# Expert stage of a six-layer decoder on one core: norm, gates and routing moved among the first shared tiles

## What is computed

```python
xn = _layernorm(x)                                  # per row
logits = xn @ gate_w.T                              # 8 experts
topk_w, topk_i = top_k(softmax(logits), 2)
topk_w = topk_w / (topk_w.sum(-1) + 1e-20) * 2.5
y = sum over the 2 chosen e of topk_w * (silu(xn @ w_gate[e]) * (xn @ w_up[e])) @ w_down[e]
out = x + y + shared_1(xn) + shared_2(xn)           # the same form of MLP, 352 wide each
```

## Time and profile before

| what | value |
|---|---|
| median of 3 runs | 4069.13 us (4068.13 to 4070.47) |
| time of the profiled execution | 4078.57 us |
| its span, first to last instruction | 4076.8 us |
| mean granted TensorE clock | 0.928 |
| busy share PE, DVE, ACT, POOL | 86%, 72%, 63%, 46% |
| this stage | from 3479.9 us of the span to its end |

### The profile page before, as it was taken

The page is one execution under the profiler, slowest core; times in us unless marked ns, Lnnn a source line. Parts: engine busy times, 40 slices in busy tenths (PEclk is TensorE's granted clock), DMA queues, the critical chain, the costliest instruction groups (busy, mean ns, idle before and its releaser), DMA issues. The chain is left out here.

```text
span 4076.8 us, 64192 instructions
## 1 busy us (share of the span) xinstructions
PE 3499.0 (86%) x22125; PEld 2796.1 (69%) x22128; DVE 2930.9 (72%) x5974; ACT 2550.4 (63%) x3361; POOL 1863.8 (46%) x1143
## 2 busy tenths in 40 slices
PE   6867623369999999999999999995889889679999
PEld 4645421247777777877778788773767667579999
DVE  4568789868878887788878888884666675434347
ACT  2334445448878887787878878872666666234433
POOL 0034410026555565565555556532766666380005
PEclk9988856689999999999999999996999999699999
DMA  1047700058878888787878878880748559432224
GB/s 49 0 94 131 143 1 1 1 139 151 143 139 147 140 149 140 139 153 139 143 138 142 151 143 155 154 155 18 134 88 152 102 91 176 166 122 90 76 77 144
DMA packets 1571360, 470.22 MB, mean 115 GB/s; under 512 B 1507174, under 2 KB 1565159, under 8 KB 1569767
## 3 DMA queue, kind: packets, MB, share of 16 engines
q1 hardware_dynamic: 1564903, 449.40, 58.0%
q0 software_dynamic: 6144, 16.79, 1.2%
HBM read 49.00 MB, written 39.58 MB: 22 GB/s over the span
## 5 line engine op out<-in xcount | busy, mean ns | idle before, releaser
L2299 DVE TENSOR_REDUCE d_neg_max<-psum 128x1 f32<-128x1024 f32 x512 | 625.1, 1221 | 249.9 <-PE psum L2040 244.1
L2189 ACT ACTIVATE psum<-psum,d_bias 128x1024 f32<-128x1024 f32 x512 | 557.6, 1089 | 336.0 <-DVE d_bias L2303 332.2
L2040 PE MATMUL psum<-d_KH,d_QH 128*128 128x512 f32 x2048 | 682.7, 415 | 19.7 <-DVE d_halves L2308 12.3
L2308 DVE SCALAR_TENSOR_TENSOR d_halves<-psum,d_halves 128x1024 f16<-128x1024 f32 x512 | 623.1, 1217 | 24.9 <-ACT d_halves L2196 22.0
L2040 PE MATMUL psum<-d_KL,d_QH 128*128 128x512 f32 x2048 | 638.1, 393 | 0.0
L2040 PE MATMUL psum<-d_KH,d_QL 128*128 128x512 f32 x2048 | 637.3, 392 | 0.0
L1999 POOL TENSOR_TENSOR d_KC<-d_KC,d_tap_of 128x1024 f32<-128x1024 f32 x126 | 301.9, 2396 | 566.0 <-ACT d_tap_of L2179 566.0
L2196 ACT ACTIVATE d_halves<-psum 128x1024 f16<-128x1024 f32 x512 | 521.8, 1019 | 3.5
L2040 PEld LDWEIGHTS psum<-d_KH,d_QH 128*128 128x128 f32 x2048 | 360.8, 189 | 131.6 <-issue 40.5
L2040 PEld LDWEIGHTS psum<-d_KL,d_QH 128*128 128x128 f32 x2048 | 385.1, 188 | 86.9
L2040 PEld LDWEIGHTS psum<-d_KH,d_QL 128*128 128x128 f32 x2048 | 385.2, 188 | 86.7
(11 more groups left out here) (513 smaller groups left out, 7606.3 us busy)
## 6 DMA issues: line engine op xcount, KB each, us to landing
f_weights_raw<-in_L_ffn_packed_dram SPq DMA_DIRECT2D x10, 1088.0 KB, 15.9
f_tile<-expert_rows SPq DMA_DIRECT2D x71, 128.0 KB, 2.2
f_expert_out<-f_tile SPq DMA_DIRECT2D x71, 128.0 KB, 1.7
d_probsT<-d_halves SPq DMA_TRANSPOSE x512, 4.3
f_tile<-f_kept_rows SPq DMA_DIRECT2D x64, 128.0 KB
expert_rows<-d_group_mixT SPq DMA_DIRECT2D x7, 1024.0 KB, 11.4
residual_stream<-in_x_dram SPq DMA_DIRECT2D x4, 1024.0 KB, 9.4
f_kept_rows<-residual_stream SPq DMA_DIRECT2D x4, 1024.0 KB, 8.6
```

Of the source, the lines that this page charges most:

```text
L2040: last = t.matmul(scores_at(u)[:, cols], q_part[:, ch, j * P:(j + 1) * P], k_part[hh % 2][:, ch, cols], start=k == 0, stop=k == 5)
L2189: a.activation(scores_at(u), scores_at(u), ACT.Exp, bias=bias[u % 2][:, 0:1])\
L2299: v.tensor_reduce(neg_max[u % 2][:], scores_at(u), AXIS.X, ALU.max, negate=True)\
L2308: v.scalar_tensor_tensor(halves[u % 4][:, 1, :], scores_at(u), LIFT, halves[u % 4][:, 0, :], ALU.mult, ALU.subtract).then_inc(probs_low.se ...
```

## The change

The two programs become one. In it:

- **SP** issues the save of batch 0, the gate weights and net 0, then the saves of batches 1 to 3 and nets 1 to 8; the loads of the kept tiles follow on the same queue. A tile is read only once its batch has been saved.
- **TensorE** does the gate work of batch 0 (`gates`) before tile 0 and that of batches 1, 2, 3 in the steps i = 1, 2, 3, ahead of `up(i)`. The transposes use the PSUM banks of g and u; logits and ranks are in bank 7, so that `y_bank` is bank 6 alone for the A tiles, and `down(k)` waits for `add_a(k-1)` in place of `add_a(k-2)`.
- **Ranks**: at i = 6 TensorE computes each row's rank over all tiles and the totals, with one matmul of 264 columns and 32 of 256 down to 8 columns, bf16. The five shifted adds, the copy and three further steps on DVE go.
- **Routing** is 38 steps in place of 48 and works on the logits; the softmax's sum and exponents come later. The steps are in DVE's i = 4 (6 steps), 5 (6), 7 (8), 8 (7), 11 (3) and 14 (8), ahead of the product of that step.
- **Splits**: ACT's high splits are at i = 0 to 5 and at 16 and 18. POOL does the low parts of nets 1 to 6 as one operation of 2176 columns each, DVE those of nets 7 and 8 in four parts at i = 18, 20, 22, 24.
- **POOL** issues its 64 scatters in one run, with no wait and no split between them, once the slots are known (end of DVE's step 8), waits for all to land, and then itself issues the loads of the first three routed tiles.

```diff
+    ON_POOL = 6
+    RANKED_AT = 6
...
-        def split_low(g, n, lo, hi):
+        def split_low(eng, n, lo, hi, done):
...
+        route_plan = {4: pick_first, 5: pick_second, 7: place_experts, 8: place_rows, 11: place_tiles,
+                      14: weigh_picks}
+        late_split = {18: (ON_POOL + 1, 0, GU), 20: (ON_POOL + 1, GU, NW), 22: (ON_POOL + 2, 0, GU),
+                      24: (ON_POOL + 2, GU, NW)}
+        high_plan = {i: i + 1 for i in range(ON_POOL)}
+        high_plan[16], high_plan[18], high_plan[R0 + 20] = ON_POOL + 1, ON_POOL + 2, E + 1
...
+            bank = 6 + (k % 2 if k > R0 else 0)
...
             @block.sync
+                save(0)
+                sp.dma_start(gate_w[:], chunked(w["gate_w"])).then_inc(gate_in.sem, 16)
+                load_net(sp, 0)
+                for b in range(1, B):
+                    save(b)
+                for n in range(1, E + 1):
+                    load_net(sp, n)
...
             @block.gpsimd
+                unit_norms(0)
+                unit_norms(1)
+                split_low(g, 0, 0, NW, weight_low)
+                unit_norms(2)
+                unit_norms(3)
...
+                for n in range(1, ON_POOL + 1):
+                    split_low(g, n, 0, NW, weight_low)
                 g.wait_ge(rows_cleared.sem, rows_cleared.at(16 * 8))
+                g.wait_ge(route.sem, route.at(PLACED))
                 for t in range(NT):
-                    g.wait_ge(upped.sem, upped.at(3 * t // 4))
                     for i in range(2):
                         g.indirect_dma_start(xs[:, :], bass.IndirectOffsetOnAxis(ap=slots[:, i, t:t + 1], axis=0),
                                              X[:, t, :], None).then_inc(spread.sem, 16)
-                    if t % 4 == 3:
-                        split_low(g, t // 4 + 1, 0, GU)
-                        split_low(g, t // 4 + 1, GU, NW)
-                split_low(g, E + 1, 0, NW)
+                g.wait_ge(spread.sem, spread.at(16 * 2 * NT))
+                for r in range(3):
+                    g.dma_start(T[3 + r][:], rows(xs, r)).then_inc(x_first[r].sem, 16)
+                split_low(g, E + 1, 0, NW, weight_low)
...
             @block.tensor
+                def gates(b, following):
+                    turn_half(b, 0)
+                    turn_x(following)
+                    turn_half(b, 1)
+                    gate_half(b, 0)
+                    gate_half(b, 1)
...
+                    t.matmul(PS[:, at:at + (NT + 1) * E], before[:], flat, start=True, stop=False)
+                    for shift in range(1, NT + 1):
+                        last = t.matmul(PS[:, at + shift * E:at + (NT + 1) * E], every[:],
+                                        flat[:, 0:(NT + 1 - shift) * E], start=False, stop=shift == NT)
...
-                    y_free(t, k - 2)
+                    y_free(t, k - 1 if k <= R0 else k - 2)
...
-                turn_x(0)
+                gates(0, 0)
                 for i in range(K + 2):
-                    if i + 1 < K:
+                    if 0 < i < B:
+                        gates(i, i + 1)
+                    elif i + 1 < K:
                         turn_x(i + 1)
...
+                    if i == RANKED_AT:
+                        rank_rows()
...
             @block.scalar
-                high_x(0)
+                split_high(a, 0)
+                keep_batch(0, 0)
...
             @block.vector
+                measure(0)
+                measure(1)
+                apply(0)
+                measure(2)
+                apply(1)
                 low_x(0)
+                measure(3)
+                apply(2)
+                low_x(1)
+                apply(3)
...
+                    if i in route_plan:
+                        route_plan[i](v)
+                    if i in late_split:
+                        split_low(v, *late_split[i], weight_low_late)
```

More of the change, by code:

```diff
@@ L3176, in stage_expert_ffn @@
     x_in, y_out = [c(f"f_x_in{i}") for i in range(3)], [c(f"f_y_out{i}") for i in range(2)]
+    x_first = [c(f"f_x_first{i}", False) for i in range(3)]
     b_in, b_out = [c(f"f_b_in{i}") for i in range(3)], [c(f"f_b_out{i}") for i in range(3)]
@@ L3213, in stage_expert_ffn @@
         hTH, hTL = place("hT_high", [P, 3, P], F32R), place("hT_low", [P, 3, P], F32R)
+        tile_at = [at + 4 * D * i for i in range(7)]
         T = [place(f"tile{i}", [P, D]) for i in range(7)]
@@ new lines, in stage_expert_ffn, with place_experts @@
+        HE = E // 2
+        end = ends[1][:, HE:HE + E]
+        def place_experts(v):
+            v.wait_ge(ranked.sem, ranked.at(1))
+            step(v, v.tensor_tensor(over[:], rank[:, NT, :].unsqueeze(2).to_broadcast([P, E, NT]),
+                                    tile_rows[:].unsqueeze(1).to_broadcast([P, E, NT]), ALU.is_gt))
+            step(v, v.tensor_reduce(tiles[:], over[:], AXIS.X, ALU.add))
+            step(v, v.tensor_copy(ends[0][:, HE:HE + E], tiles[:]))
+            for i in range(3):
+                shift, old, new = 1 << i, ends[i % 2], ends[(i + 1) % 2]
+                step(v, v.tensor_tensor(new[:, HE:HE + E], old[:, HE:HE + E], old[:, HE - shift:HE - shift + E],
+                                        ALU.add))
+            step(v, v.tensor_tensor(first_tile[:], end, tiles[:], ALU.subtract))
+            step(v, v.tensor_scalar(first_row[:], first_tile[:], float(P), None, ALU.mult))
@@ L3290, in place_tiles, with place_rows @@
+        def place_rows(v):
+            step(v, v.tensor_tensor(where[:], rank[:, 0:NT, :], per_expert(first_row[:]), ALU.add))
+            for i in range(2):
+                step(v, v.tensor_tensor(cell[:], pick[i][:], where[:], ALU.mult))
+                step(v, v.tensor_reduce(slot_f[i][:], cell[:], AXIS.X, ALU.add))
+                step(v, v.tensor_copy(slots[:, i, :], slot_f[i][:]))
+        def place_tiles(v):
             step(v, v.tensor_tensor(passed[:], tile_number[:].unsqueeze(2).to_broadcast([P, ROUTED, E]),
@@ new lines, in _ @@
+                unit_norms(0)
[3 more added lines that the diff above has]
+                unit_norms(3)
+                g.memset(before_f[:], 1.0).then_inc(const_built.sem, 1)
+                g.memset(every[:], 1.0).then_inc(const_built.sem, 1)
+                g.memset(chosen[:, NT, :], 0.0).then_inc(const_built.sem, 1)
+                for i in range(2):
+                    g.memset(ends[i][:, 0:E // 2], 0.0).then_inc(const_built.sem, 1)
```

343 lines of the change are left out of this document (147 added, 196 removed).

## The result

The changed kernel takes 4109.23 us (median of 4, 4099.26 to 4113.27) against 4069.8 us for the kernel before on the same chip (4068.13 to 4071.3): ratio 1.0088, with a 95% interval of 1.0071 to 1.0104. It is slower by 0.9%, where 4056 us and a gain were forecast.

What follows compares the result with a forecast made beforehand. It took a 66.8 us prelude without tiles, a TensorE-bound tile loop and 28 us of ScalarE stops as bounds. Its terms summed to 169.8 us plus 28, 197.8 against 210.6 to tile 32's turn: 4056 us, range 4028 to 4100.

Steps and rivals of the forecast that it cites:

- item 8: ScalarE's stops during GpSimd's 81 us run of 64 scatters: 28 us taken; bounds nothing, 28, or the run's whole rest.
- rival B: One long scatter run holds ScalarE to its end: slower, 235.6 us to tile 32's turn, 4094 us; chance 0.34.
- Item 6: VectorE's routing work beside GpSimd's splits, blocked on two-input SBUF reads: 3 us taken, bounds 0 and 9.7.
- item 3: Gate batches 1 to 3 on TensorE, now ahead of tiles: 8.5 us a batch, 25.5 us in all (22.2 to 34.8).
- item 4: The 33 rank matmuls on TensorE: 3.0 us taken, no more than 3.9, waiting for nothing.
- Item 1: From the stage's start to the first gate transpose: 8.2 us, as before.
- Item 2: Batch 0's gate work with the turns of tiles 0 and 1: 11.7 us; tile 0's up matmuls add 1.6.
- Item 5: VectorE's routing steps, 0.46 us each, beside its tile work: 3 us too many (0 to 4).
- C: No ScalarE stops in the scatter run: 173.3 us to tile 32's turn, 37 less, 4032 us; chance 0.20.
- the rule behind it: Trainium skill: DMA never contends with a compute engine and ScalarE never waits on anyone, so the run's length is no matter.
- D: Gates hide nothing: TensorE stays at half its clock, splits block VectorE; 213.8 us, 4072 us, no difference; chance 0.08.
- What would show it: The prediction's list of trace signs for the forecast and its rivals, such as tile 32 turned near 198 us.

Runs made afterwards that it cites:

- e2_plain: Changed kernel with each of the 64 scatters made a plain DMA of the same tile, issued by GpSimd to rows of its own; 4026.7 us, one run.
- e1_landings: Changed kernel with GpSimd waiting after every fourth scatter until all have landed; 4072.3 us, ratio 1.0005 to the kernel before.
- the mended version: Changed kernel with splits kept clear of VectorE's long work and a wait for landing after each eighth or sixth scatter; ratios 0.9957 and 0.9940.

## Why the prediction was wrong

**The step that failed is item 8,** "The ACT stops", as the sum put it: "I take 28", if what a scatter costs ACT is the same in the long run as in the short ones. The hold is worth 248.3 - 171.5 = 76.8 us. The ends that the prediction gave (nothing, 28, the rest of the run) held the truth, and rival B named the mechanism with 235.6 to 245 us; the value was chosen by the wrong row. The stops of 3 to 5 us were read as a price per scatter (0.44 us each), but each was cut off by the end of its run. A stop that always ends with its cause tells nothing of how long it would last. Seven of eight runs ended so; that weighed more than the single instruction that got through inside one. B should have been the likeliest, at its upper end.

One reading under it was wrong too: "what it waits for is there". In the trace of before the up matmuls of the earlier trace rows end at 3629.96, but the event of their semaphore is recorded at 3634.78, and the silu starts at 3634.80. The stops were late signals of TensorE there as well. It would not have given the price.

**The rest of the sum came out near, by luck: its errors cancel.** Without item 8 the forecast was 169.8 us; e2_plain, without the hold, has 171.5. Item 6 was some 10 us too low, item 3 was 5 us too high and item 4 about 1. By its items:

- Item 1: 8.2; the first gate transpose comes at 3472.05, 8.25 us after the start.
- Item 2: 11.7; from there to tile 0's up matmuls at 3484.36 it is 12.3.
- Item 3: 8.5 a batch; 6.5, 7.8 and 6.0 us (3488.03 to 3494.49, 3501.79 to 3509.55, 3514.54 to 3520.57), 20.3 in sum and not 25.5.
- Item 4: 3.0 for 33 rank matmuls; 32 of them took 2.05 us.
- Item 5: the six route steps of step 5 took 2.74 us, 0.46 each.
- Item 6: 3 taken, 0 to 9.7 as bounds. In step 4 alone it was 4.50 + 4.87 - 0.84 = 8.5 us, near the upper bound; and the scalings of batch 3 (11.65 us), which the item did not count, made TensorE wait 4.43 us more. TensorE's granted clock, 1.00 just before, was 0.63 in the stop and 0.79 in the 12 us behind it (windows below). Undoing both gave 14.5 us up to the first scatter. The rule of the Trainium skill (SBUF - State Buffer, "Who interferes with whom") that was set against the item, up to 9.7 us, came nearer to the 8.5 than the row chosen.

```profile
3525.00:3530.00 5.00, 5.00 (x39) 4.98 (x38) 3.88 (x9) 3.84 (x7) 1.62 (x1) 1.00 0.08 26
3532.00:3539.00 7.00, 0.00 (x0) 0.00 (x0) 6.93 (x4) 0.00 (x0) 6.23 (x2) 0.63 0.00 0
3539.00:3551.00 12.00, 11.31 (x86) 11.07 (x87) 7.23 (x19) 2.46 (x6) 0.00 (x0) 0.79 0.15 45
```

**Rivals.** C and the rule behind it: the time of 171.5 to 173.3 us exists, but in these runs only when the DMAs are not indirect. D: the gates come cheaper than forecast, eight transposes taking 1.04 us in batch 3 where they took 1.94 in batch 0; but DVE was blocked by the splits as D had it. "What would show it" was of use: the sign named for B, ScalarE empty for over 60 us and the clock down, is what the windows show.

**One slip in the reading** stood in the expectations of e2_plain: the three loads at the end of GpSimd's run are one group of 1.71 us, not 1.71 us each. A row's "x3" has to be divided out.

## What to carry to other kernels

Don't let GpSimd issue indirect DMAs back to back beside a pipeline in which other engines wait for TensorE: put something of 1.7 us or more (a wait for landing, a piece of its own work) after each four to six. When an engine stands though its producer's row has long ended, look for the semaphore's event: the row's end isn't yet the signal. A stall that ends whenever its cause ends has no known length; when a change makes the cause longer, price the stall at the cause's full length until a run says otherwise. And before work is moved beside other work, list which of VectorE's instructions read two tiles of SBUF, scale in place or copy, and what GpSimd does in that time.

## What the runs showed of the hardware that was not expected

- 64 indirect DMAs 1.27 us apart hold ScalarE for about 77 us, at 1 KB a row and at 128 bytes a row; 64 plain ones from GpSimd, 0.54 us apart at 310 GB/s, do not. What comes late is TensorE's semaphore events, 58 us behind the matmul's row for the copy at 3641.49 in the changed kernel; TensorE's own matmuls drift apart, and VectorE goes on until it needs ScalarE.
- The hold per run of indirect DMAs, estimated from the lengths: 0.3 us for four (e1_landings), 1.3 to 1.6 us for six, almost 6 for eight (3.5 with the longer breaks of the kernel before), 77 for 64. The usual 0.3 us between two of them does not end it, with or without a memset inside.
- A VectorE instruction with two SBUF inputs, or a copy in SBUF, that meets a split is stopped for what is left of it, however small it is: 2.28 us for a copy of 8 columns. A reduction beside the same split is not.
- Open: what delays TensorE's signals. No row names it, and no run takes the indirect form apart further than its bytes and the number under way. Whether the mended version gains from still earlier scatters was not tried.
